# Scores of the first network's local attention: three products per head and group in place of four

## The chip, the cores and the metric

The kernel runs on one core of a Trainium2 chip. The metric is the time of the whole program on the device, in microseconds (us); lower is better. Inside the core five engines work side by side: TensorE (PE; its weight loads are listed apart as PEld), VectorE (DVE), ScalarE (ACT), GpSimd (POOL), and SyncE (SP), which here only starts transfers.

## The reference, cut to what matters

The program is a chain of four residual layers over 16 batches of 128 tokens with 128 channels: a cross attention, a network of 6 layers (the first network), a second cross attention, and a network of 2 layers (the second network). The change touches only the local attention of the first network, with 16 heads of 64 channels and a window of 32:

```python
bq = q.reshape(b, h, nw, w, d)                 # w = 32 queries of a window
bk2, bv2 = (look(bk), look(bv))                # keys of the window before and of this one
mask = (it < jb) | (it > jb + w) | (jb == -1)
sim = jnp.einsum('bhwie,bhwje->bhwij', bq, bk2) * QK_SCALE
sim = jnp.where(mask, -jnp.finfo(sim.dtype).max, sim)
attn = jax.nn.softmax(sim, -1)
```

With 128 tokens there are four windows of 32 queries. A query of the first window sees up to 32 keys, one of the other three up to 64 (its own window and the one before).

## The kernel before

All work is written out by hand for each engine as one long list; semaphores order the engines against each other. The first network runs as 96 passes (6 layers x 16 batches). A pass is cut into two units of 8 heads (i = 0 and 1), so there are 192 units. Step s of the loop (step_0) works on several passes at once: it projects queries and keys of pass s (L710), turns them for pass s - 1 (L731), does the scores of unit 0 for pass s - 1 and of unit 1 for pass s - 2, and later turns the probabilities (L776), multiplies by the values (L790) and projects out (L823). The feed-forward work of a group of four batches is spread over four steps (24 groups); in one of the four ACT evaluates the Gelus (L1631), for which it loads another table, and then goes back to the evictions of the value products (L1609) and the exponents of the scores (L1578).

The scores of a unit are made by scores_all, called twice in each step (from step_0). Each call is followed on PE by the value products of a unit (values_all, L790). Eight heads stand as four head numbers j in two groups g; group g has its channels on partitions 64 g to 64 g + 63 and its scores in PSUM bank 3 + g, one row per query, 64 key slots per head. Slot n of a query is key 32 (window - 1) + n, for the first window key n.

First the mask is written: for each block of 32 queries and each group a bf16 product of a piece of the identity (64 x 32) with mask_b over 256 columns (four heads x 64 slots), L761. It opens the accumulation. Then for each head number, each piece of queries and each group an fp32 product adds the scores, L767; on PE an fp32 product is two matmuls, each with its own weight load. The pieces are (first query, first key, number of keys), always with 32 queries, so the stationary tile is always 64 rows x 32 columns of the array. Slots 32 to 63 of the first window get the mask's -1e30 and no product. The last product raises AT["s"], on which DVE takes the row maximum (L2195).

The mask table in DRAM (mask_by_slot) and its copy in SBUF hold all 64 slots of all 128 queries. In the second network a function of its own (scores) uses 64x64 tiles for mask (L741) and products (L747).

Of the kernel before, what the change touches and what calls it, by code (L numbers as in the profile page):

```python
# [14 lines left out]
P = 128  # L15
# [5 lines left out]
DH = 64  # L21
# [42 lines left out]
def build(nc, A, out):  # L64
# [9 lines left out]
    with ExitStack() as ctx:  # L74
        sb = lambda name, shape, dt=F32: ctx.enter_context(nc.sbuf_tensor(name, shape, dt))
        sem = lambda name: ctx.enter_context(nc.semaphore(name))
        bank = [ctx.enter_context(nc.psum_tensor(f"bank{i}", [P, BLK], F32)) for i in range(8)]
# [4 lines left out]
        ident_b = sb("ident_b", [P, P], BF16)  # L82
# [3 lines left out]
        mask_b = [sb("mask_b0", [P, 2, 4, DH], BF16), sb("mask_b1", [P, 2, 4, P], BF16)]  # L86
# [50 lines left out]
        q_t = [slot(18 + i) for i in range(2)]  # L137
        k_t = [slot(20 + i) for i in range(2)]
# [437 lines left out]
        def _(pe):  # L576
# [125 lines left out]
            def pe_phase(ph):  # L702
# [48 lines left out]
                def scores_all(i, p):  # L751

                    if p == 0:
                        pe.wait_ge(YP["we"], 2)
                    pe.wait_ge(AT["qte"][i], p + 1)
                    pe.wait_ge(AT["kte"][i], p + 1)
                    for q in range(0, P, 32):
                        for g in range(2):
                            rows = slice(DH * g, DH * g + DH)
                            own = ident_b[rows, DH * g + q % DH:DH * g + q % DH + 32]  # L760
                            nc.tensor.matmul(bank[3 + g][q:q + 32, 0:256], own, mask_b[0][rows, q // DH], start=True, stop=False)  # L761
                    pieces = [(0, 0, 32), (32, 0, 64), (64, 32, 64), (96, 64, 64)]
                    for j in range(4):
                        for q, key, n in pieces:
                            for g in range(2):
                                rows = slice(DH * g, DH * g + DH)
                                mm = nc.tensor.matmul(bank[3 + g][q:q + 32, DH * j:DH * j + n],  # L767
                                                      q_t[i][rows, P * j + q:P * j + q + 32], k_t[i][rows, P * j + key:P * j + key + n],
                                                      start=False, stop=j == 3)
                    mm.then_inc(AT["s"], 1)  # L770

# [174 lines left out]
                def step_0(s):  # L946
# [32 lines left out]
                    if live(s - 2):  # L979
                        at(pe, AG["ex"][0][0], s - 1)  # L980
                        at(pe, AG["ex"][0][1], s - 1)
                        scores_all(1, s - 2)
# [43 lines left out]
                    if live(s - 1):  # L1026
                        at(pe, AT["kte"][0], s)
                        turn(1, s - 1, 1, "mk", "kt")
                        if live(s - 2):
                            at(pe, AG["pte"][0][0], s - 1)  # L1030
                        else:
                            at(pe, AT["qte"][0], s)
                        turn(1, s - 1, 0, "mq", "qt")
                        if live(s - 2):
                            at(pe, AG["ex"][1][0], s - 1)
                            at(pe, AG["ex"][1][1], s - 1)
                        scores_all(0, s - 1)
# [1660 lines left out]
```

## Time and profile before

| | |
|---|---|
| time, median of 3 runs | 2304.53 us (2298.14 to 2307.23) |
| time of the profiled execution | 2299.02 us |
| its span, first to last instruction | 2297.2 us |
| mean granted TensorE clock | 0.987 |
| PE busy | 2124.9 us, 93%, 33,790 matmuls |
| PEld busy | 1456.7 us, 63%, 33,790 weight loads |
| DVE, ACT, POOL busy | 1760.9 (77%), 1712.2 (75%), 1340.2 us (58%) |
| HBM read and written | 23.11 MB, 1.05 MB |

The span is what the instructions take from the first to the last; the time of the execution lies 1.8 us above it. Busy times are unions, so two matmuls that overlap on PE count once. Ends of matmuls are modelled by the profiler, their starts are recorded; distances are therefore read here from start to start. "issue" behind an idle time means that the profile shows nothing that ended it.

### The profile page before, as it was taken

What the parts mean: (1) busy time and instruction counts of PE and PEld (TensorE: products, weight loads), DVE (VectorE), ACT (ScalarE), POOL (GpSimd) and SP (SyncE); (2) the same over time, 40 slices, a digit from 0 to 9 for tenths busy, and PEclk for the clock granted to TensorE, in tenths of its full rate; (3) what the DMA queues carried; (4) which work ended last, traced back from release to release, by engine and by line L of the source; (5) the groups of instructions that cost most, each with busy time, mean ns of one, the idle gap of its engine ahead of it and who ended that gap; (6) DMA issues with size and microseconds to landing.
All of it is one profiled execution on the core that took longest, in us unless ns stands there. A gap on an engine that the chain in (4) does not pass through costs nothing. (4 is left out here: it accounts for less than half of the span.)

```text
span 2297.2 us, 88445 instructions
## 1 busy us (share of the span) xinstructions
PE 2124.9 (93%) x33790; PEld 1456.7 (63%) x33790; DVE 1760.9 (77%) x4953; ACT 1712.2 (75%) x5916; POOL 1340.2 (58%) x1270
## 2 busy tenths in 40 slices
PE   7988999999999999999999999999999886899997
PEld 5656666666666666666666666666666564666665
DVE  4988877778777878777778777877777478788873
ACT  3767788787787877787887777887788543778784
POOL 1337666666666666665676566666666124766660
PEclk8999999999999999999999999999999998999999
DMA  4001221112211222112211122111221100000001
GB/s 112 4 3 39 70 58 45 41 46 67 57 43 39 64 51 57 39 43 61 57 46 42 43 65 60 46 39 45 52 53 43 48 10 10 13 13 16 13 9 28
DMA packets 144799, 96.93 MB, mean 42 GB/s; under 512 B 61976, under 2 KB 137408, under 8 KB 144384
## 3 DMA queue, kind: packets, MB, share of 16 engines
q1 hardware_dynamic: 143232, 91.02, 15.5%
q8 instruction: 274, 4.49, 0.8%
q14 instruction: 141, 1.16, 0.2%
q10 hardware_dynamic: 1152, 0.26, 0.1%
HBM read 23.11 MB, written 1.05 MB: 11 GB/s over the span
## 5 line engine op out<-in xcount | busy, mean ns | idle before, releaser
L710 PE MATMUL bank<-wqkv,hs 128*128 128x512 f32 x1344 | 666.7, 614 | 19.3 <-ACT arena L1609 13.7
L1931 POOL TENSOR_TENSOR arena<-arena,rnorm 128x512 f32<-128x512 f32 x448 | 455.5, 1046 | 388.5 <-DVE rnorm L2180 387.3
L1924 POOL TENSOR_TENSOR arena<-arena 128x512 f32<-128x512 f32 x448 | 568.0, 1275 | 132.5 <-DVE arena L2129 132.2
L1578 ACT ACTIVATE arena<-bank,amx 128x64 f32<-128x64 f32 x1536 | 458.8, 336 | 8.5 <-DVE amx L2195 8.3
L2124 DVE TENSOR_TENSOR arena<-bank,rot 128x512 f32<-128x512 f32 x448 | 306.9, 685 | 82.7 <-PE bank L710 79.0
L1555 ACT ACTIVATE arena<-bank 128x512 f32<-128x512 f32 x448 | 264.4, 617 | 132.0 <-PE bank L731 130.9
L710 PEld LDWEIGHTS bank<-wqkv,hs 128*128 128x128 f32 x1344 | 228.6, 191 | 203.8 <-issue 154.9
L1578 ACT ACTIVATION_READ_ACCUMULATOR arena<-bank,amx 128x1 f32 x1536 | 352.3, 229 | 0.0
L2129 DVE TENSOR_TENSOR arena<-bank,rot 128x256 f32<-128x256 f32 x896 | 334.0, 414 | 0.0
L731 PEld LDWEIGHTS bank<-ident,arena 128*128 128x128 f32 x1792 | 212.6, 142 | 152.8 <-issue 128.3
L2136 DVE TENSOR_REDUCE ss<-arena 128x8 f32<-128x512 f32 x448 | 283.4, 670 | 32.5 <-ACT arena L1549 32.3
L1549 ACT ACTIVATE arena<-bank 128x512 f32<-128x512 f32 x448 | 265.9, 647 | 42.0 <-DVE arena L2129 41.2
L1938 POOL TENSOR_TENSOR arena<-arena,ainv 128x512 f32<-128x512 f32 x192 | 200.7, 1045 | 164.9 <-DVE ainv L2203 164.7
L731 PE MATMUL bank<-ident,arena 128*128 128x128 f32 x1792 | 251.5, 274 | 14.1 <-POOL arena L1931 6.4
L1609 ACT ACTIVATE arena<-bank 128x256 f32<-128x256 f32 x384 | 127.2, 387 | 174.6 <-PE bank L790 173.7
L823 PEld LDWEIGHTS bank<-arena,wo 128*128 128x128 f32 x1792 | 221.6, 194 | 55.1 <-issue 48.1
L790 PE MATMUL bank<-arena 64*64 64x32 f32 (+1 forms) x9216 | 186.1, 221 | 49.0 <-issue 47.6
L823 PE MATMUL bank<-arena,wo 128*128 128x128 f32 x1792 | 226.9, 279 | 3.0 <-ACT arena L1609 2.6
L790 PEld LDWEIGHTS bank<-arena 64*64 64x64 f32 x9216 | 160.6, 134 | 71.0 <-issue 54.5
L2195 DVE TENSOR_REDUCE amx<-bank 128x4 f32<-128x256 f32 x384 | 143.8, 416 | 39.8 <-PE bank L767 39.2
L767 PE MATMUL bank<-arena 64*32 64x64 f32 (+1 forms) x12288 | 168.8, 217 | 0.0
L767 PEld LDWEIGHTS bank<-arena 64*32 64x32 f32 x12288 | 154.9, 105 | 0.3
(213 smaller groups left out, 3229.8 us busy)
## 6 DMA issues: line engine op xcount, KB each, us to landing
arena<-arena SPq DMA_DIRECT2D x768, 64.0 KB
wqkv<-in_L_ffn_Wqkv_dram SPq DMA_DIRECT2D x24, 256.0 KB
hs<-z SPq DMA_DIRECT2D x128, 32.0 KB, 1.8
hs<-z SPq DMA_DIRECT2D x128, 31.8 KB, 1.9
fx<-z SPq DMA_DIRECT2D x31, 128.0 KB, 2.2
fx<-z SPq DMA_DIRECT2D x31, 127.0 KB, 2.5
wqkv<-in_L_ffn_Wqkv_dram SPq DMA_DIRECT2D x24, 128.0 KB
w<-in_L_ffn_W_dram SPq DMA_DIRECT2D x6, 341.0 KB
```

The lines of the kernel that those rows point to most:

```text
L710: nc.tensor.matmul(bank[o][:], src[:], wqkv[w][:, off:off + 512], start=True, stop=True).then_inc(AT[name] if part < 2 else AT[name][i], 1)
L731: mm = nc.tensor.transpose(bank4[o][:, j, :], rc[i][c][p % 2][:, j * P:(j + 1) * P], ident[:])
L767: mm = nc.tensor.matmul(bank[3 + g][q:q + 32, DH * j:DH * j + n], q_t[i][rows, P * j + q:P * j + q + 32], k_t[i][rows, P * j + key:P * j + ...
L790: mm = nc.tensor.matmul(bank4[7 - half][to:to + DH, j, q0:q1], src[g][rows, DH * h:DH * h + DH], pbt[i][0][rows, h * P + q0:h * P + q1], s ...
L823: mm = nc.tensor.matmul(bank4[7][:, 0, :], wo[w][:, i, j, :] if ni == 0 else wo[w][:, j // 2, j % 2, :], o_t[i][:, j * P:(j + 1) * P], sta ...
L1549: nc.scalar.activation(sq[i][c], bank[c][:], ACT.Square).then_inc(AT["sqk" if c else "sqq"], 1)
L1578: ins = nc.scalar.activation(pb[i][0][p % 2][:, h * DH:(h + 1) * DH], bank[3 + g][:, j * DH:(j + 1) * DH], ACT.Exp, bias=amx[p % 2][:, i, ...
L1924: nc.gpsimd.tensor_tensor(t, t, rs[i][c], ALU.add).then_inc(AT["ak" if c else "aq"][i], 1)
L1931: nc.gpsimd.tensor_tensor(t, t, rnorm[p % 2][:, i, HU * c:HU * c + HU].unsqueeze(2).to_broadcast([P, HU, DH]), ALU.mult).then_inc(AT["mk" ...
L2124: nc.vector.tensor_tensor(heads(rc[i][c][p % 2]), src, r[:, 2 * c, :].unsqueeze(1).to_broadcast([P, HU, DH]), ALU.mult)
L2129: ins = nc.vector.tensor_tensor(dst, src[:, :, (1 - a) * hd:(2 - a) * hd], r[:, 2 * c + 1, a * hd:(a + 1) * hd].unsqueeze(1).to_broadcast( ...
L2136: nc.vector.tensor_reduce(ss[:, i, HU * c:HU * c + HU], heads(sq[i][c]), AX.X, ALU.add).then_inc(AT["ssk" if c else "ssq"], 1)
```

## The change

Queries 0 to 63 of a head are multiplied in one product with keys 0 to 63 on a tile of 64 x 64, in place of two products with 32 queries each. Queries 64 to 95 and 96 to 127 keep their tiles of 64 x 32 and their 64 keys. Slots 32 to 63 of the first window now get a product on top of the mask's -1e30. The mask is written by four products with 64 x 64 tiles in place of eight with 64 x 32 tiles. The order of heads, pieces and groups, the waits and the semaphore at the end stay. Nothing else in the program changes.

```diff
--- before.py
+++ after.py
@@ -754,18 +754,17 @@
                         pe.wait_ge(YP["we"], 2)
                     pe.wait_ge(AT["qte"][i], p + 1)
                     pe.wait_ge(AT["kte"][i], p + 1)
-                    for q in range(0, P, 32):
+                    for q in range(0, P, DH):
                         for g in range(2):
                             rows = slice(DH * g, DH * g + DH)
-                            own = ident_b[rows, DH * g + q % DH:DH * g + q % DH + 32]
-                            nc.tensor.matmul(bank[3 + g][q:q + 32, 0:256], own, mask_b[0][rows, q // DH], start=True, stop=False)
-                    pieces = [(0, 0, 32), (32, 0, 64), (64, 32, 64), (96, 64, 64)]
+                            nc.tensor.matmul(bank[3 + g][q:q + DH, 0:256], ident_b[rows, rows], mask_b[0][rows, q // DH], start=True, stop=False)
+                    pieces = [(0, DH, 0), (64, 32, 32), (96, 32, 64)]
                     for j in range(4):
-                        for q, key, n in pieces:
+                        for q, m, key in pieces:
                             for g in range(2):
                                 rows = slice(DH * g, DH * g + DH)
-                                mm = nc.tensor.matmul(bank[3 + g][q:q + 32, DH * j:DH * j + n],
-                                                      q_t[i][rows, P * j + q:P * j + q + 32], k_t[i][rows, P * j + key:P * j + key + n],
+                                mm = nc.tensor.matmul(bank[3 + g][q:q + m, DH * j:DH * j + DH],
+                                                      q_t[i][rows, P * j + q:P * j + q + m], k_t[i][rows, P * j + key:P * j + key + DH],
                                                       start=False, stop=j == 3)
                     mm.then_inc(AT["s"], 1)
 
```

## Rows read from the trace of the kernel before

**Rows 1.** Stages: length, busy time of each engine (count), granted clock, DMA; first network.
```profile
core 0: us, PE busy (x) PEld busy (x) DVE busy (x) ACT busy (x) POOL busy (x), PEclk, DMA share, GB/s
176.00:1808.00 1632.00, 1540.22 (x28604) 1063.56 (x28591) 1273.24 (x3731) 1291.66 (x4732) 1051.89 (x982) 0.99 0.20 50
```

**Rows 2.** What PE waited for, 200 to 1800 us: total us, times, longest.
```profile
PE bank L790 <- issue: 47.6, 65, 3.1
PE bank L761 <- issue: 19.4, 22, 1.0
PE bank L710 <- ACT arena L1609: 13.7, 16, 0.9
```

**Rows 3.** Timeline of PE over one unit.
```profile
start us, us, engine line op out<-in xcount [idle before <-releaser]
1008.54 0.60 PE L731 MATMUL bank<-ident,arena 128*128 128x128 f32 x4
1009.07 0.30 PE L761 MATMUL bank<-mask_b,ident_b 64*32 64x256 bf16 x8
1009.19 0.84 PE L767 MATMUL bank<-arena 64*32 64x32 f32 x64
1009.96 0.90 PE L790 MATMUL bank<-arena 64*64 64x64 f32 x48
```

**Rows 4.** Timeline of the weight loads over the same unit.
```profile
1009.07 0.11 PEld L761 LDWEIGHTS bank<-mask_b,ident_b 64*32 64x32 bf16 x8 [0.17 <-issue]
1009.09 0.77 PEld L767 LDWEIGHTS bank<-arena 64*32 64x32 f32 x64
1009.96 0.79 PEld L790 LDWEIGHTS bank<-arena 64*64 64x64 f32 x48
```

**Rows 5.** Groups by line and shape, whole span: count, busy us, mean ns, idle before.
```profile
L767 PE MATMUL bank<-arena 64*32 64x64 f32 x9216 | 167.2, 223 | 0.0
L767 PE MATMUL bank<-arena 64*32 64x32 f32 x3072 | 126.7, 197 | 0.0
```

**Rows 6.** Timeline of PE where one tile shape follows itself.
```profile
1016.98 0.60 PE L731 MATMUL bank<-ident,arena 128*128 128x128 f32 x4
1017.41 0.60 PE L776 MATMUL bank<-ident,arena 128*128 128x128 f32 x4
```

**Rows 7.** Timeline of PE in narrow windows: last transpose, last score matmul.
```profile
1008.87 0.27 PE L731 MATMUL bank<-ident,arena 128*128 128x128 f32 x1
...
1009.82 0.22 PE L767 MATMUL bank<-arena 64*32 64x64 f32 x1
```

**Rows 8.** Timeline of weight loads in the second network: mask, scores.
```profile
2050.67 0.11 PEld L741 LDWEIGHTS bank<-mask_b,ident_b 64*64 64x64 bf16 x4 [0.17 <-issue]
2050.70 1.01 PEld L747 LDWEIGHTS bank<-arena 64*64 64x64 f32 x32
```

**Rows 9.** Stretches of L790: length, PE (matmuls in it), PEld (loads in it), clock.
```profile
1009.95:1010.06 0.11, 0.10 (x4) 0.10 (x8) 1.00 0.00 0
1010.06:1010.10 0.04, 0.04 (x8) 0.04 (x12) 1.00 0.00 0
```

**Rows 10.** DMA queue 8 (packets, MB, share); timeline of PE with two stalls.
```profile
q8 instruction: 274, 4.49, 0.8%
...
1059.63 0.30 PE L761 MATMUL bank<-mask_b,ident_b 64*32 64x256 bf16 x8 [0.57 <-issue]
...
1063.13 0.86 PE L790 MATMUL bank<-arena 64*64 64x64 f32 x24 [1.82 <-issue]
```

**Rows 11.** Timelines of ACT and PE in a step with Gelus.
```profile
985.16 1.28 ACT L1631 ACT_TABLE_LOAD   x1
...
988.99 1.12 PE L710 MATMUL bank<-wqkv,hs 128*128 128x512 f32 x2 [0.87 <-ACT arena L1609]
...
992.82 0.30 PE L761 MATMUL bank<-mask_b,ident_b 64*32 64x256 bf16 x8 [0.98 <-issue]
```

**Rows 12.** A stretch of the first network, columns as in rows 1.
```profile
1062.80:1069.50 6.70, 6.37 (x38) 4.23 (x38) 2.88 (x7) 3.99 (x20) 1.28 (x1) 0.50 0.15 40
```

## Prediction

> **What bounds the kernel now.** I read the stages first. In the stage of the first network, which holds all 192 calls that the change touches (96 batches, two units each), PE is busy for 1540.2 of 1632 us; ACT has 1291.7, DVE 1273.2 and POOL 1051.9 [rows 1]. The other two stages run none of the changed lines. PE's waits come next: by the ends that the profile models PE stands idle for 47.6 us ahead of the value products (L790), put down to nothing that the profile shows, for 19.4 us ahead of the mask (L761) and 13.7 us ahead of the projections (L710) [rows 2]. The rest of the stage PE goes from one block of matmuls straight to the next, so a microsecond added to or taken from PE's own work there moves the end by about a microsecond, less what comes out of those waits.
>
> Third, one unit on PE in order of time: transposes, mask, 64 score matmuls (an fp32 product is two of them), value products. From the first mask matmul at 1009.07 to the first value product at 1009.96 a unit's scores take 0.89 us, of which the mask is 0.12 [rows 3]. Fourth, the weight loads of the same stretch, because they show what paces it: the 64 loads of the scores start at 1009.09, 0.10 us ahead of the first score matmul at 1009.19, run beneath the mask and take 0.77 us with no gap put down before them. The mask's own loads behave otherwise: they start at 1009.07, together with their matmul, after 0.17 us in which the load side stood still [rows 3, 4]. The reader is to see this difference: between mask and scores nothing stops, between transposes and mask something does.
>
> **The change part by part.** *Counts.* Per unit the products go from 4 heads x 4 pieces x 2 groups = 32 to 24, 64 matmuls to 48; the mask from 8 to 4. Over 192 units L767's 9216 + 3072 matmuls [rows 5] become 9216: 3072 on a 64x64 tile, 6144 on 64x32. The streamed columns of a tile's longest line don't change (four heads x 64 columns, twice).
>
> *What the tile's width costs.* The old unit uses 64x32 tiles for mask and scores throughout. The new one issues, in each head, two 64x64 products and then four 64x32 products, so the width alternates: 1 change in the first head, 2 in each of the other three, 7 inside the unit. The changes at its two ends (128x128 into it, 64x32 to 64x64 out of it) stay in number. What is one change worth? Four transposes followed by four transposes start 0.43 us apart: 0.108 each, hence 0.054 for 64 columns [rows 6]. Four transposes followed by the mask take 0.53 [rows 3]; the last of them starts at 1008.87 and the mask at 1009.07, 0.20 us later [rows 7]. That is 0.09 more than its own 0.108. The last score matmul starts at 1009.82 [rows 7] and the first value product at 1009.96 [rows 3], 0.14 later, of which its own streaming is 0.054: again 0.09. This second place is the very change of width (64x32 to 64x64, same 64 rows) that the new code makes inside a head. Where the tile stays, as between 64x64 mask and 64x64 scores of the second network, the loads start 0.03 us behind the mask's first and no stop is put down [rows 8]. So a change of tile shape empties the array: what was issued must stream out, about 0.09 us more passes, and only then does the next weight load start.
>
> The Trainium skill's TensorEngine Tiling (Array Packing), section Tiling Modes, says that changing the mode, as opposed to the tile, drains TensorE; it lists 64x64 and 64x32 as two modes. By that all seven changes would stop, where my rows only show changes between blocks; the sum by it is the one below.
>
> *The sum of a unit with stops.* Besides the 0.14 from last start to next first start, each short block now pays its own two passes one behind the other. After the change to 64x64 tiles four value matmuls start by 1010.06, and the second passes join between 1010.06 and 1010.10, about 0.11 after the first ones [rows 9]: the streaming of 0.054 and as much again for the exposed load of 64 columns. A block of 32-wide tiles is not in the trace by itself; its second pass lies between 0.054 (load fully hidden) and 0.11. I take 0.08, half the load, and 0.02 for issuing four tiles instead of two. So a 64x32 block costs 0.14 + 0.08 + 0.02 = 0.24 and a 64x64 block 0.14 + 0.11 + 0.01 = 0.26. From the mask's start: first score matmul 0.12, its second pass 0.18, then four blocks of 0.24 and three of 0.26: the last score matmul starts at 1.92 and the values at 2.06, against 0.89. That is 1.17 us more per unit, 225 us over 192.
>
> *What it gives back.* First, L790's 47.6 us. PE's instructions arrive in packets of 16 KB (274 of them on queue 8, 4.49 MB), which is 247 of the 67,580 loads and matmuls per packet; a stall such as the 1.82 us in the middle of a unit's value products, while PE waits for no engine, I read as PE having run ahead of its packets [rows 10]. One unit now issues 128 score loads and matmuls, 16 for the mask and 96 for the values in 1.7 us. After the change it issues 200 in 2.9 us, and any 247 would need over 4 us; the stalls of up to 3.1 us go. I take all 48; bounds 0 and 48. Second, in each of the 24 steps with the Gelus ACT loads its table anew (1.28 us) ahead of them, and PE then waits 0.87 us for L1609's eviction and 0.98 ahead of the following mask [rows 11]. The scores of that step run before these waits and ACT's work does not depend on their end, so 1.17 us more of PE work only fills the waits: 24 x 1.17 = 28 us; bounds 0 and 44. No edit adds a wait on a semaphore. Behind longer scores stand DVE's row maximum and ACT's exponents, which PE next needs before the following scores; PE's own work in between is unchanged, so they are no later against PE than now.
>
> 225 - 48 - 28 = +149 us. The profiled execution took 2299.0 us (span 2297.2), so 2448; its median of three lies 5.5 us higher, hence **2453 us**.
>
> *Bounds.* Low: each change costs only its 0.09 (7 x 0.09 x 192 = 121 us) and the whole give-back holds: +45, 2350. High: blocks of 0.28 and the first 0.18, so 2.28 instead of 0.89, 267 us, nothing given back: 2572.
>
> **The rivals.** *Widths mix freely (ends faster).* The stop might belong to the boundary of two blocks of code and not to the width, or the array might stop only a tile that is still in use. For it: every stop that I read stands between different lines. Against it: blocks of one shape follow each other with no stop [rows 6, 8], and the first value products wait for the last score matmul of the other tiles too. Then fewer loads would decide: 64 loads of 32 columns take 0.77 us, 12.0 ns each, and 48 of 64 columns 0.79, 16.5 ns [rows 4]; 16 x 16.5 + 32 x 12.0 = 0.65, so 0.12 us less per unit, 23 us, plus half to all of L790's stalls, since 200 instead of 240 instructions fill such a burst: -47 to -71, minus some 10 that ACT then holds up. About 2255, at the outside 2235 to 2292. It decides as soon as a change inside a head costs under 0.02 us.
> The Trainium skill's TensorE: Matmul & The Clock Gate, Part 3, prices packed tiles at the matmul's duration plus about 4 ns for each further tile. Estimated from that page, 16 fewer matmuls would give 64 ns per unit, 12 us, on the same side as this rival; the trace's 12 ns per load speaks for a larger step.
>
> *The clock falls.* In 1062.8 to 1069.5 the granted clock was 0.50, 1.2 instead of 2.4 GHz [rows 12], after PE had been idle for 0.57 us ahead of 1059.63 and 1.82 ahead of 1063.13 [rows 10]. The new units hold 7 stops; where the clock falls once in each of the 96 steps for half such a stretch (3.4 us, losing 1.7), 163 us come on top: 2616. It decides if the stops count as idleness; against it, of a block's 0.25 us the array streams 0.11, so a unit has some 1.1 us of emptiness in small parts where those two idle times were 2.39 us, and with all its other stalls the stage's clock was 0.99 [rows 1].
>
> **How the numbers follow.** Stops at each change 0.86; free mixing 0.09; falling clock 0.05. The range takes the first case with nearly all of its bounds, 2365 to 2560; what lies outside is the other two cases and thin ends, under 2 in 10. A measurement of this kernel tells apart some 0.5% (11.5 us). Faster 0.08 (free mixing, nearly whole), same 0.02, slower 0.90.
>
> **What would show it.** Right: L767 (one line higher) with 9216 matmuls whose loads come in groups of four and eight, each behind a gap put down to nothing; mask to values near 2.06 us per unit; L790's wait far below 47.6; PE fuller, ACT, DVE and POOL with lower shares; the clock near 0.99. Wrong: loads of the scores still in one uninterrupted row of about 0.65 us (free mixing); a granted clock of 0.5 through much of the stage (third case); L790's stalls still there, which would add up to 48 us; block lengths other than 0.24 to 0.26, each 0.01 us of which is 13 us in the sum.

## The result and the profile after

The changed kernel takes 2437.39 us (median of 4 runs, 2433.75 to 2441.08), the kernel before 2305.88 us (4 runs, 2298.14 to 2307.26). The ratio is 1.0582, with a 95% interval of 1.0554 to 1.0609: 5.8% slower. The forecast was 2453 us, 2365 to 2560, slower with a chance of 0.90, so it was right in direction and in size. The profiled execution of after took 2439.36 us (span 2437.6), that of before 2299.02 us: a difference of 140.3 us, where the sum said 149.

First the page of after: busy time and share of each engine, the granted clock in 40 slices, the instruction queue.

```profile
PE 2331.9 (96%) x29950; PEld 1571.8 (64%) x29950; DVE 1773.1 (73%) x4953; ACT 1710.7 (70%) x5916; POOL 1343.4 (55%) x1270
...
PEclk9989999999999999999999999999999998999999
...
q8 instruction: 244, 4.00, 0.7%
```

Then the stage of the first network (columns as in rows 1), which now ends 140 us later, at 1948 (both ends are cut just behind the last mask, which starts at 1806.9 in before and at 1947.0 in after).

```profile
176.00:1948.00 1772.00, 1747.09 (x24704) 1178.54 (x24699) 1283.55 (x3720) 1289.73 (x4731) 1054.99 (x982) 0.99 0.18 46
```

Beside rows 1, ACT, DVE and POOL have the same work as before, within 1% (ACT 1289.73 against 1291.66). PE has 3840 matmuls fewer over the whole program (29,950 against 33,790) and is busy 207 us longer in the stage, 98.6% of it against 94.4%. The mean granted clock is the same 0.99. So the time is added on PE, in its own work, and hardly by the clock. The whole difference between the stages is PE's.

PE's waits in 200 to 1940 us (total, times, longest) and the timeline of one unit, against rows 2 and 3:

```profile
PE bank L760 <- issue: 21.5, 22, 1.0
PE bank L822 <- ACT arena L1608: 0.9, 1, 0.9
PE bank L710 <- ACT arena L1608: 0.8, 1, 0.8
```

```profile
start us, us, engine line op out<-in xcount [idle before <-releaser]
988.07 0.30 PE L760 MATMUL bank<-mask_b,ident_b 64*64 64x256 bf16 x4
988.20 2.05 PE L766 MATMUL bank<-arena 64*64 64x64 f32 x48
990.17 0.90 PE L789 MATMUL bank<-arena 64*64 64x64 f32 x48
```

The 47.6 us ahead of the value products are off the list. The 13.7 us ahead of the projections are down to 0.8. The wait ahead of the mask stays (19.4, now 21.5). And from the mask's start to the values' a unit now takes 2.10 us instead of 0.89. Where these 2.10 us are is seen in the weight loads of the scores, cut at the blocks' borders (length of the stretch, busy time of the loads with their number, clock, DMA share, GB/s). A load that reaches over a border counts on both sides, so the loads that start in a stretch are 4 or 8:

```profile
988.20:988.41 0.21, 0.14 (x5) 1.00 0.29 78
988.41:988.66 0.25, 0.16 (x10) 1.00 0.00 0
988.66:988.92 0.26, 0.19 (x6) 1.00 0.00 0
988.92:989.17 0.25, 0.16 (x10) 1.00 0.24 70
989.17:989.43 0.26, 0.19 (x6) 1.00 0.66 166
989.43:989.68 0.25, 0.16 (x10) 1.00 0.09 16
```

The old loads ran in one row of 0.77 us [rows 4]. The new ones go in blocks of four (64 columns wide) and eight (32 wide), and every block takes about a quarter of a microsecond, whatever its size. These are the stops that the prediction counted. Over all 768 changes from 64x64 to 64x32, the first load of the new shape starts 0.147 us (median) behind the last matmul of the old one, over the 576 changes back 0.144 us; the load side stands still for 0.067 and 0.092 us of it. So no load starts early over a change of shape. That the array is empty at that moment is a reading of this: the recorded starts do not show it, and the ends of matmuls are modelled.

**Where the time went.** I summed PE's time over all 192 units from the start of each block to the start of the next, so that a wait belongs to the block that it interrupts or follows.

| us | before | after | difference |
|---|---|---|---|
| mask and scores | 184.6 | 406.1 | +221.5 |
| value products | 221.3 | 166.2 | -55.1 |
| everything else | 1882.7 | 1856.2 | -26.5 |
| sum | | | +139.9 |

### The profile page after: what moved, and what is told of

It reads as the page before. It is cut to its first block and busy times, and to the rows that moved or that the text cites. A ratio compares the mean times of both kernels' runs of the same rounds, so it can differ in the third digit from the quotient of the medians.

```text
span 2437.6 us, 80765 instructions
## 1 busy us (share of the span) xinstructions
PE 2331.9 (96%) x29950; PEld 1571.8 (64%) x29950; DVE 1773.1 (73%) x4953; ACT 1710.7 (70%) x5916; POOL 1343.4 (55%) x1270
## 5 line engine op out<-in xcount | busy, mean ns | idle before, releaser
L710 PE MATMUL bank<-wqkv,hs 128*128 128x512 f32 x1344 | 670.2, 619 | 4.8 <-ACT arena L1548 2.5
L766 PE MATMUL bank<-arena 64*32 64x64 f32 (+1 forms) x9216 | 394.4, 231 | 0.0
L1577 ACT ACTIVATION_READ_ACCUMULATOR arena<-bank,amx 128x1 f32 x1536 | 358.2, 233 | 0.0
L710 PEld LDWEIGHTS bank<-wqkv,hs 128*128 128x128 f32 x1344 | 232.1, 194 | 185.2 <-issue 152.3
L766 PEld LDWEIGHTS bank<-arena 64*32 64x32 f32 (+1 forms) x9216 | 278.5, 114 | 104.9 <-issue 0.5
L1937 POOL TENSOR_TENSOR arena<-arena,ainv 128x512 f32<-128x512 f32 x192 | 200.5, 1044 | 184.8 <-DVE ainv L2202 184.7
L822 PEld LDWEIGHTS bank<-arena,wo 128*128 128x128 f32 x1792 | 217.9, 192 | 55.1 <-issue 48.2
L789 PE MATMUL bank<-arena 64*64 64x32 f32 (+1 forms) x9216 | 175.9, 222 | 0.7 <-ACT arena L1597 0.7
L789 PEld LDWEIGHTS bank<-arena 64*64 64x64 f32 x9216 | 154.6, 136 | 19.7 <-ACT arena L1597 1.5
```

The lines of the kernel that those rows point to most:

```text
L710: nc.tensor.matmul(bank[o][:], src[:], wqkv[w][:, off:off + 512], start=True, stop=True).then_inc(AT[name] if part < 2 else AT[name][i], 1)
L766: mm = nc.tensor.matmul(bank[3 + g][q:q + m, DH * j:DH * j + DH], q_t[i][rows, P * j + q:P * j + q + m], k_t[i][rows, P * j + key:P * j + ...
L789: mm = nc.tensor.matmul(bank4[7 - half][to:to + DH, j, q0:q1], src[g][rows, DH * h:DH * h + DH], pbt[i][0][rows, h * P + q0:h * P + q1], s ...
L822: mm = nc.tensor.matmul(bank4[7][:, 0, :], wo[w][:, i, j, :] if ni == 0 else wo[w][:, j // 2, j % 2, :], o_t[i][:, j * P:(j + 1) * P], sta ...
L1577: ins = nc.scalar.activation(pb[i][0][p % 2][:, h * DH:(h + 1) * DH], bank[3 + g][:, j * DH:(j + 1) * DH], ACT.Exp, bias=amx[p % 2][:, i, ...
```

## The experiments

The theory: each change of tile shape empties the array, and from the last start of one block to the first start of the next about 0.14 us pass, of which 0.054 us would have passed without a change. Its rivals: the width itself is dear (wide loads, or the mask's tiles), or the added keys are; the gain on the value products is not from instruction packets; a clock that falls under the stops.

All kernels by the number of changes of shape (inside the unit, between the mask's first product and the last score product):

| kernel | changes inside | mask to values, median per unit, us | mask and scores, us | values, us | median time, us | ratio to before [95%] |
|---|---|---|---|---|---|---|
| before | 0 | 0.957 | 184.6 | 221.3 | 2298.8 to 2305.9 | |
| keys_only | 0 | 0.962 | 184.8 | 222.0 | 2304.27 | 1.0011 [0.9992, 1.0029] |
| narrow_only | 0 | 1.032 | 201.6 | 213.5 | 2304.88 | 1.0028 [1.0012, 1.0044] |
| shift | 0 | 0.964 | 185.4 | 218.8 | 2306.30 | 1.0034 [1.0013, 1.0055] |
| mask_only | 1 | 1.002 | 197.7 | 208.7 | 2300.52 | 0.9987 [0.9968, 1.0006] |
| narrow_first | 1 (none at the end) | 1.084 | 221.2 | 175.7 | 2281.13 | 0.9908 [0.9879, 0.9936] |
| one_change | 1 | 1.272 | 245.2 | 176.4 | 2300.52 | 0.9993 [0.9971, 1.0014] |
| after | 7 | 2.109 | 406.1 | 166.2 | 2437.39 | 1.0582 [1.0554, 1.0609] |
| narrow_mask | 8 | 2.263 | 435.3 | 164.6 | 2460.90 | 1.0701 [1.0683, 1.0719] |
| per_group | 15 | 3.983 | 795.1 | 243.2 | 3105.36 | 1.3508 [1.3481, 1.3535] |

### The same products with one change of shape inside

The products of after, all 64x64 ones of the four heads first, then all 64x32 ones:

```diff
-                    for j in range(4):
-                        for q, m, key in pieces:
+                    for part in (pieces[:1], pieces[1:]):
+                        for j in range(4):
+                            for q, m, key in part:
```

> The products of the changed kernel in another order: the 64x64 products of all four heads first, then the 64x32 products of all four. As many instructions and the same tiles, but one change of width inside a unit in place of seven. If the change of width costs the time: from the mask's start the first score matmul at 0.13 us, eight passes of 0.055 on the wide tiles, one change (0.15), eight passes on the narrow ones, values at about 1.27 us against 2.11 in the changed kernel and 0.96 in the kernel before; +0.31 us per unit, +59 us over 192, and the 55 us of stalls in the value products stay gone with some 15 of other waits: 2285 to 2310 us, about as the kernel before. If the wide tile itself were slow (its loads or its products), the order would not matter: about 2437 us. If only the number of instructions counted, it would be faster than before by 20 to 60 us whatever the order.

Measured: 2300.52 us, ratio 0.9993 [0.9971, 1.0014]; clock 0.989. One unit on PE:

```profile
990.62 0.30 PE L760 MATMUL bank<-mask_b,ident_b 64*64 64x256 bf16 x4
990.75 1.21 PE L767 MATMUL bank<-arena 64*64 64x64 f32 x48
991.89 0.90 PE L790 MATMUL bank<-arena 64*64 64x64 f32 x48
```

The same 48 score matmuls, the same mask, keys and bytes as after, in another order. With six changes fewer a unit takes 1.27 us instead of 2.10. The sums of mask and scores differ by 160.9 us, 0.838 us per unit, 0.14 per change. (This 0.14 is the whole price of a change: some 0.09 us of stop beyond the streaming, and some 0.05 because a short block's second passes no longer follow at the usual distance. That it equals the distance over a stop is chance.) That takes the blame from the wide tiles and the added keys: the median of after lies 136.9 us above this one, and this one is level with before, so the whole net loss goes with the order. Against before, the scores are still 60.6 us dearer, and the values (-44.9) and the rest (-12.5) give back 57.4. One change is at most 28 us of the 60.6 (0.148 us, 192 times). Another part is that products of one shape now go out in 16 passes, some 0.056 us apart, each on half of the array's tiles, where before has eight passes over all eight tiles: narrow_only below has such passes without any change of shape, and its mask and scores are 17.0 us dearer. How the remainder divides no run separates.

### One change inside and none at the end

Mask in narrow tiles as before, 64x32 products first, then the 64x64 ones, which the value products follow in the same shape:

```diff
-                    for q in range(0, P, DH):
+                    for q in range(0, P, 32):
...
-                    for j in range(4):
-                        for q, m, key in pieces:
+                    for part in (pieces[1:], pieces[:1]):
+                        for j in range(4):
+                            for q, m, key in part:
```

> As the one before, but the mask in eight 64x32 tiles, then the 64x32 products of all heads, then the 64x64 products of all heads, so that the value products (64x64) follow with no change of width: one change inside the unit, none at its end. If the change of width costs the time: mask 0.12 us, eight passes 0.4, change 0.15, eight passes with an exposed first load 0.45, values at about 1.16 us against 0.96 before; +38 us over 192 units, less 55 for the stalls in the value products and some 15 of other waits: 2265 to 2290 us, faster than both. If the order does not matter: about 2437 us. If the stalls in the value products are not tied to how many instructions PE consumes in a short time, they stay and it takes about 2330 us.

Measured: 2281.13 us, ratio 0.9908 [0.9879, 0.9936]. This is faster than both kernels, and 0.9% faster than the kernel before. One unit, and PE's waits in 200 to 1760 us:

```profile
993.21 0.30 PE L761 MATMUL bank<-mask_b,ident_b 64*32 64x256 bf16 x8
993.34 1.16 PE L768 MATMUL bank<-arena 64*32 64x64 f32 x45
994.29 0.27 PE L791 MATMUL bank<-arena 64*64 64x64 f32 x1
994.34 0.23 PE L768 MATMUL bank<-arena 64*64 64x64 f32 x2
994.40 0.84 PE L791 MATMUL bank<-arena 64*64 64x64 f32 x46
```

```profile
PE bank L761 <- issue: 20.9, 22, 1.0
PE bank L710 <- ACT arena L1610: 12.6, 18, 0.7
PE bank L791 <- issue: 9.3, 12, 1.7
```

The last scores and the first values stand interleaved: two lines of code, one tile shape, no stop. In before the same place takes 0.14 us [rows 3, 7]. So the stop belongs to the shape and not to the border of two blocks of code, the doubt that the prediction's first rival rested on. This kernel has as many changes as before, only elsewhere. Its mask and scores are 36.6 us dearer than before's (again 16 passes on half of the tiles each), and it wins because the values lose 45.6 us and the rest 12.2: -21.2 in all, where the profiled executions differ by 20.3.

### The mask alone in wide tiles

Before, with the mask loop of after (four 64x64 products); the scores stay four 64x32 pieces:

```diff
-                    for q in range(0, P, 32):
+                    for q in range(0, P, DH):
```

> The kernel before with the mask alone changed: four 64x64 mask products, then the old four pieces on 64x32 tiles. One change of width inside a unit, eight instructions fewer per unit. If the change of width costs the time: the first score matmul 0.21 to 0.24 us after the mask's start in place of 0.12, +0.1 us per unit, +20 us, little of it given back: 2315 to 2330 us. If not: fewer instructions and the same time or up to 5 us less, 2298 to 2306 us.

Measured: 2300.52 us, ratio 0.9987 [0.9968, 1.0006]. PE, then the weight loads, of one unit:

```profile
1000.22 0.30 PE L760 MATMUL bank<-mask_b,ident_b 64*64 64x256 bf16 x4
1000.46 0.84 PE L766 MATMUL bank<-arena 64*32 64x32 f32 x64
1001.26 0.90 PE L789 MATMUL bank<-arena 64*64 64x64 f32 x48
...
1000.45 0.68 PEld L766 LDWEIGHTS bank<-arena 64*32 64x32 f32 x64
```

The loads of the scores start 0.23 us behind the mask, where in before they started 0.02 behind it [rows 4]: one stop, +22.1 us in the sum of the mask. But the expected 20 us or so are not in the time. The scores behind the stop got 8.9 us shorter and the values 12.6, with fewer stalls (31.7 us ahead of them by the waits of 200 to 1760 us, 45.8 in before). Mask and scores are 13.1 us dearer, the end is level. I had taken a stop as a price that is simply added, and that expectation missed. Behind the stop the median unit's scores take 0.77 us, as long as in the quickest units of before (0.891 less 0.120): what went is the small stalls that most of the old units have in their scores. Why they went was not tested.

### The keys alone

Before, with 64 keys for the first window:

```diff
-                    pieces = [(0, 0, 32), (32, 0, 64), (64, 32, 64), (96, 64, 64)]
+                    pieces = [(0, 0, 64), (32, 0, 64), (64, 32, 64), (96, 64, 64)]
```

> The kernel before with 64 keys instead of 32 for the first window on its old 64x32 tile: the added columns alone, no change of width, no instruction more or fewer. The tile's line becomes as long as the other seven tiles' lines. If the columns of a tile run beside the others: 2300 to 2312 us, no change. If added columns cost in sequence: 8 products x 2 passes x 32 columns x 0.42 ns = 0.21 us per unit, +41 us, 2345 us.

Measured: 2304.27 us, ratio 1.0011 [0.9992, 1.0029]. Groups by shape, where rows 5 had two:

```profile
L767 PE MATMUL bank<-arena 64*32 64x64 f32 x12288 | 169.0, 222 | 0.0
```

Mask and scores take 184.8 us instead of 184.6. The added columns cost nothing, as the prediction had them. (By 0.054 us for 64 columns [rows 6] the other case would have cost some 82 us and not 41; neither came.)

### The mask narrow, the products as in after

After, with before's mask loop, so that the change from 64x32 (mask) to 64x64 (first head) comes on top: 8 changes.

```diff
-                    for q in range(0, P, DH):
+                    for q in range(0, P, 32):
```

> The changed kernel with the old mask in eight 64x32 tiles: the products alone are changed. Eight changes of width inside a unit, four mask products more. If each change costs what the trace shows: the first 64x64 product 0.21 to 0.24 us after the mask's start in place of 0.13 and its second pass 0.05 later still, +0.13 us per unit, +25 us: 2455 to 2470 us. If the mask's width had a part in the loss, it would be faster than the changed kernel.

Measured: 2460.9 us, ratio 1.0701 [1.0683, 1.0719]. One unit:

```profile
1000.73 0.30 PE L761 MATMUL bank<-mask_b,ident_b 64*32 64x256 bf16 x8 [0.82 <-issue]
1000.96 2.10 PE L767 MATMUL bank<-arena 64*64 64x64 f32 x48
1002.99 0.90 PE L790 MATMUL bank<-arena 64*64 64x64 f32 x48
```

From mask to scores 0.23 us, in after 0.13. The sum of mask and scores grows by 29.2 us, 0.152 per unit, for one change more; values and rest give 7.0 back. The ratio grows from 1.0582 to 1.0701, some 27 us with an uncertainty of about 7, and the profiled executions lie 22.5 apart, so most of it arrives at the end.

### Groups apart: 15 changes

After, with the loops over groups and pieces swapped:

```diff
-                        for q, m, key in pieces:
-                            for g in range(2):
+                        for g in range(2):
+                            for q, m, key in pieces:
```

> The changed kernel with the two groups of a head one after the other: one 64x64 product, two 64x32 products, then the same for the other group. The same instructions, 15 changes of width inside a unit in place of 7. Blocks of 0.25 us (64x64) and 0.24 us (64x32): 0.98 per head in place of 0.51, +1.9 us per unit, +365 us: 2780 to 2810 us, some 20 less if the last waits of PE are filled too. If tiles that don't overlap let each other run, the group order would not matter: 2437 us.

Measured: 3105.36 us (2 runs), ratio 1.3508 [1.3481, 1.3535]. The stage, the granted clock in 40 slices, and one unit:

```profile
176.00:2600.00 2424.00, 2418.70 (x24653) 1598.54 (x24652) 1299.84 (x3697) 1308.29 (x4713) 1053.07 (x982) 0.85 0.13 34
...
PEclk9988888888888888888888888888888888999999
...
1004.75 0.30 PE L760 MATMUL bank<-mask_b,ident_b 64*64 64x256 bf16 x4
1004.89 3.92 PE L766 MATMUL bank<-arena 64*64 64x64 f32 x48
1008.74 1.51 PE L789 MATMUL bank<-arena 64*64 64x64 f32 x48
```

The unit's length came as expected, 3.98 us. Against after that is 0.23 per added change, more than 0.14, since the two groups of a piece no longer run side by side. The time did not: it is some 300 us above what this length gives at full clock. The granted clock of the stage is 0.85; by its records TensorE ran at 1.2 instead of 2.4 GHz in 156 stretches, 784 us in all, 146 of them in the stage. PE has hardly a pause there that the profile shows (busy for 2418.70 of 2424 us); from the first mask on, 143 of 147 stretches begin within a unit's scores, where the stops lie, or less than 0.9 us behind them. That also stretches lines that nobody changed:

```profile
L710 PE MATMUL bank<-wqkv,hs 128*128 128x512 f32 x1344 | 863.8, 775 | 5.0 <-ACT arena L1548 2.5 <-ACT arena L1611 1.2 <-ACT arena L1608 0.8
```

A projection takes 775 ns on the mean, against 619 in after. The mean clock of the execution is 0.874 with 15 changes per unit and 0.986 with 7 (after) and 8 (narrow_mask). But it falls with 7 as well, only seldom: in the stage of after seven stretches at 1.2 GHz begin, 23.9 us in all, in that of before three (17.1 us). The waits and the clock at the first of them:

```profile
320.18 0.30 PE L760 MATMUL bank<-mask_b,ident_b 64*64 64x256 bf16 x4 [0.98 <-issue]
...
322.40:325.80 3.40, 3.40 (x51) 2.30 (x52) 1.14 (x4) 2.14 (x14) 1.64 (x2) 0.50 0.26 67
```

All seven begin right behind the scores of a unit that had come after the wait of up to 0.98 us ahead of the mask. There are 21 or 22 such waits in every kernel but per_group; a fall follows within 4.5 us on seven of them in after, on three in narrow_mask, and on none to two in each of the others (on one in before, where a stall of 1.82 us comes on top [rows 10]). With per_group, where hardly a wait is seen, this says that many stops bring the clock down. From how many on it falls in most units is open.

### Order and number of instructions apart

The value products lost most or all of their stalls in every kernel with three pieces. To see whether the order or the smaller number of instructions does it: before, its mask and its 64 score matmuls kept, pieces 2 and 3 of all heads first, then 0 and 1. No width changes.

```diff
-                    for j in range(4):
-                        for q, key, n in pieces:
+                    for part in (pieces[2:], pieces[:2]):
+                        for j in range(4):
+                            for q, key, n in part:
```

> The kernel before with its old mask and its four old pieces, in another order: first the pieces of queries 64 to 127 for all heads, then those of queries 0 to 63 for all heads. No 64-wide tile, no change of width inside the unit, all 64 + 8 matmuls, four tiles at work at a time as in the run with the narrow products first. It tells whether that run gained by its order or by its fewer instructions. If by fewer instructions (the stalls in the value products): first matmul 0.134 us after the mask, 16 passes of 0.056, values at 1.12 us against 0.96 before, +31 us, and most of the 45 us of stalls remain because a unit's scores and values are still 240 loads and matmuls, in a little longer a time: 2310 to 2335 us. If the regular order itself were the gain: about 2280 us.

Measured: 2304.88 us, ratio 1.0028 [1.0012, 1.0044]. One unit, and the wait of the value products in the stage:

```profile
1004.62 0.30 PE L761 MATMUL bank<-mask_b,ident_b 64*32 64x256 bf16 x8
1004.75 0.97 PE L768 MATMUL bank<-arena 64*32 64x64 f32 x64
1005.65 0.90 PE L791 MATMUL bank<-arena 64*64 64x64 f32 x48
...
PE bank L791 <- issue: 35.8, 41, 2.6
```

The order by itself gains nothing: it makes a unit 0.075 us longer by the median and keeps three quarters of the stalls. (The unit was expected at 1.12 us and came at 1.032, and the time lies below the expected 2310 to 2335 us.) narrow_first, with 208 loads and matmuls in the burst instead of 240, has 9.3 us of them.

### Do the stalls belong to the instruction packets?

Numbering PE's records of before in their order (loads, matmuls and the semaphore instructions between them), all 47 gaps of over 0.2 us between the starts of two value products stand at the same place, number 192 or 193 counted modulo 256; numbered by loads and matmuls alone they have no common place. A packet is 4.49 MB / 274 = 16.4 KB [rows 10], and PE's 70,338 records fill 274 packets of 256; in after, 62,658 records fill 244, which is again the number of packets on queue 8. If this is a matter of packets, then work added far ahead must move the stalls to other units and leave their sum. The edit adds 32 transposes ahead of the first network, which write the same values again:

```diff
-                    for i in range(4):
-                        mm = nc.tensor.transpose(bank4[3 + g][:, i, :], yw_in[:, 4 * g + i, :], ident[:])
+                    for i in range(4 * 5):
+                        mm = nc.tensor.transpose(bank4[3 + g][:, i % 4, :], yw_in[:, 4 * g + i % 4, :], ident[:])
```

> The kernel before with 16 extra copies of four transposes in each of the two groups of the second cross attention's weights, before the first unit: 128 loads and matmuls more, half of one 16 KB instruction packet. If the stalls in the value products come from instruction packets (each PE stall of the kernel before stands at a PE record whose number is 192 more than a multiple of 256), they move to other units: none stays in the units that stalled, and the units numbered 13, 18, 22, 23, 32, 36, 51, 65, 74, 78, 79, 88, 92, 107, 121, 125, 130, 135, 144, 148, 163 and 177 stall in their place; their sum stays at 40 to 60 us; the time is 2302 us plus 7 for the extra transposes, 2295 to 2320. If they come from a semaphore or a transfer of data, they stay in the same units (11, 20, 25, 34, 39, 48, 53, 62, 81, 90, 95, 104, 109, 118, 137, 146, 160, 165, 174).

Measured: 2306.30 us, ratio 1.0034 [1.0013, 1.0055], of whose 7.5 us the added transposes are 3.5 (x40 in place of x8, 4.5 us busy in place of 1.0). Their group, and the wait of the values:

```profile
L699 PE MATMUL bank<-ident,yw_in 128*128 128x128 f32 x40 | 4.5, 272 | 0.0
...
PE bank L790 <- issue: 42.6, 64, 1.7
```

The list of units named above is not the one that came: it counted 128 added records, and there are 64, as the edit adds 32 transposes, each one load and one matmul. The test itself came out for the packets. Of the 49 units that now stall only 3 are among the 47 of before, where keys_only and narrow_only, with as many records as before and other work, share 45 and 44. All 49 gaps stand again at 192 or 193 modulo 256; they lie where a shift by 64 moves that place (45 exactly, four one or two records beside it). By the waits their sum is 42.6 us against 47.6. So the stalls are tied to a place in the stream of instructions, every 256 records, and not to the work done there.

The trace also has the time of each packet on queue 8. In the stall of rows 10, the packet runs from 1060.52 to 1061.70 us, and PE goes on at 1063.13. All 47 stalls of before end like this, 1.2 to 1.6 us (median 1.40) behind the landing of a packet, although packets land some 7.5 us apart. In the 23 other units that have such a place among their value products, PE passes it 1.5 to 6.6 us behind the landing (median 2.7), and in after, where nothing stalls, 1.7 to 10.6 (median about 6). So PE stands where the next packet comes late.

What goes with the stalls is how fast PE takes its records. The shortest time for 240 loads and matmuls is 1.72 us in before, 1.86 in narrow_only, 2.32 in mask_only, 3.77 in narrow_first, 4.95 in one_change and 5.79 in after; the gaps of over 0.2 us sum to 54.7, 47.2, 42.4, 12.9, 9.4 and 0 us. Number and time were not varied one without the other.

## Why the prediction was right

**The bound held.** In the stage of the first network PE went from 94.4 to 98.6%, the work of the other engines stayed, and what came on PE's path came at the end, less what came out of its waits.

**The stops came as read.** All 1344 changes of width inside the units of after stop the stream of loads and matmuls: 768 from 64x64 to 64x32 with a median of 0.148 us from last start to next first start, 576 back with 0.146 us; 0.14 was forecast, read from a change between two blocks of code. The median starts of a unit, counted from the mask, in us:

```
64x64 block  0.133  second passes from 0.189
64x32 block  0.341  second passes from 0.421
64x64 block  0.587  second passes from 0.693
64x32 block  0.848  second passes from 0.928
...
last score matmul 1.963, first value product 2.109
```

A 64x64 block with its change is 0.26 us (forecast 0.26), a 64x32 block 0.25 (forecast 0.24). The second pass of the narrow block comes 0.080 behind the first, as taken; that of the wide one 0.106 (0.11 taken). The last score was put at 1.92 and stands at 1.963, the values at 2.06 and stand at 2.109. The rule of the Trainium skill's TensorEngine Tiling (Array Packing), section Tiling Modes, that a change of mode drains TensorE, agrees with the trace: 0.145 us or more every time, although both shapes keep 64 rows.

**The baseline of a unit was the shortest one.** The 0.89 us of the unit shown [rows 3] is what the quickest tenth of the units takes (0.891); the median is 0.957 and the mean 0.961, because small stalls lie in the old scores too. Over an undisturbed unit the change costs 2.109 - 0.891 = 1.218 us, 234 us in all: 9 more than my 225. But the old scores lost 13.5 us in stalls (0.961 - 0.891, times 192) that I had not counted and that have gone, so mask and scores together rose by 221.5. Two small errors cancelled.

**The give-back, first term.** L790's stalls: -48 forecast, -55.1 measured in the values' blocks. The reason, PE running ahead of its packets of instructions, is borne out by shift and by the landings of the packets. The argument that 247 loads and matmuls would need over 4 us held: the shortest time for them in the stage of after is 6.2 us. The size was read from ends that the profile models. From start to start the values' blocks of before stand 61.6 us above 192 times their median of 0.832 us, those of after 6.5. The bound of a full give-back was the right end to take.

**The give-back, second term.** -28 forecast, -26.5 measured in all other blocks, 10.0 of it at L710. In the Gelu step the mask of unit 0 follows the mask of unit 1 by 8.49 us in both kernels. The stretch between them (columns as in rows 1), before and after:

```profile
984.33:992.82 8.49, 6.65 (x137) 3.94 (x137) 4.96 (x19) 8.43 (x26) 5.45 (x6) 1.00 0.13 33
```

```profile
988.07:996.56 8.49, 7.51 (x118) 4.54 (x117) 4.96 (x18) 8.43 (x26) 4.29 (x5) 1.00 0.13 33
```

ACT is busy for 8.43 of the 8.49 us both times and, by this, sets the length; PE's 0.86 us more went into its own waits. In all 22 Gelu steps that lie between two masks this distance is 8.49 us in both kernels, so the mechanism is right; the other two of the 24 come behind the last scores, where nothing could be given back. I had the place in part wrong: beyond L710's wait, 0.30 of the 0.98 us ahead of the mask was to be filled as well, and that wait stayed (21.5 us against 19.4). What ends that wait the profile does not name. Over these 22 stretches mask and scores add 24.9 us, which come out of the projections (-16.9) and of the value products (-10.0); other lines add 2.0. So 10.0 us of the first term's stalls lie where ACT sets the length, and there the two terms share one time. And the -26.5 of all other blocks is not this term alone: outside these stretches L710 gains 6.5, L849 loses 7.1 and L823 3.7. That it comes so near to -28 is in part luck.

**The sum.** 225 - 48 - 28 = 149 stands against 221.5 - 55.1 - 26.5 = 140 (rounded). The remaining 7 us of the 16 by which 2453 was too high is the step from one execution to the median: the profiled execution of before lay 6.9 us below the later median of 4, but that of after 2.0 above its own, and I had added 5.5 to the profiled time.

**The rivals.** Free mixing is refuted for this chip's tiles by all 1344 changes. The estimate from the span rule (the Trainium skill's TensorE: Matmul & The Clock Gate, Part 3), some 12 us faster, has the wrong sign here, since it leaves out the drain; the kernel with one change and none at the end is 21 us faster than before (2281.13 against 2302.18 in the same series), but through the stalls, which the rule does not contain, and with scores that are dearer. The falling clock came with 7 changes in seven single stretches, 23.9 us at 1.2 GHz in the stage against 17.1 in before, which leaves the stage's mean at 0.99 where the rival had one in each of 96 steps; with 15 it came in 146 stretches (0.85 in the stage). So the stops do count, and the argument from the small parts of emptiness was right in size for after and would have been wrong for twice as many stops.

## What to carry to other kernels

Before packing products of different tile shapes, write down the sequence of shapes as PE will see it and count the changes, across the borders of code blocks too: here 0.14 to 0.15 us passed over each from start to start, and sorting the same 48 matmuls by shape took 137 us out of the kernel. Where blocks must differ, put the same shapes of neighbouring blocks next to each other, as narrow_first does. For a short block repeated many times, compare the quickest, the median and the mean before pricing an edit by one instance from a timeline.

## What the runs showed of the hardware that was not expected

- Waits that the profile puts down to nothing can be tied to the place in PE's stream of instructions: all 47 gaps of over 0.2 us in before's value products stand at one place modulo 256 records, and 64 records added ahead move them to other units with the sum little changed (47.6 to 42.6 us by the waits). These waits shrink when a burst of 240 loads and matmuls in 1.7 us becomes 208 (9.3 us in narrow_first), and vanish when the burst is slower (after). Each of the 47 ends 1.2 to 1.6 us behind the landing of a packet on queue 8.
- One stop was free on balance: mask_only pays 22.1 us for it and gets 8.9 from the scores and 12.6 from the values back.
- With 15 stops in a unit TensorE's granted clock falls to 0.85 in the stage and lengthens unrelated products from 619 to 775 ns, while PE shows hardly a wait; with 8 it is 0.986 over the execution, against 0.987 in before. With 7 it falls in seven stretches, each behind a wait of up to 0.98 us and a unit with stops.
